# Two transformer layers: row maxima moved SBUF to SBUF, expert weights rounded by GpSimd, and an output projection moved into the tail of linear attention

## The reference

```python
# layer 0: softmax attention with alibi, 16 heads of 32
xn = layernorm(x)
q, k, v = split(xn @ Wqkv + bqkv, 3)
scores = q @ k.T / sqrt(32) - slope[h] * (i - j), causal
att = softmax(scores) @ v
x = x + att @ Wo + bo + moe(xn)            # two experts, W0a/W0b and W1a/W1b, top 1
# layer 1: linear attention with decay, gate and group norm
xn = layernorm(x)
q, k, v = silu(xn @ Wq), silu(xn @ Wk), silu(xn @ Wv)
S_t = exp(ld) * S_{t-1} + k_t v_t^T;  o_t = q_t S_t
o = o * sigmoid((xn @ Wg1) @ Wg2)
o = o * rsqrt(mean(o*o per head) + eps) * norm_w
x = x + o @ Wo + glu(xn)                   # glu with weights rounded to -1, 0, 1
```

## Time and profile before

| | us |
|---|---|
| median of 3 runs | 1733.5 (1728.63 to 1733.7) |
| the profiled execution | 1733.02, span 1731.2, mean granted clock 0.955 |
| TensorE busy in the span | 1556.5 (90%) |
| VectorE, ScalarE, GpSimd busy | 989.4, 603.2, 647.9 |
| attention | 167.4 to 805 |
| linear attention | to 1474.5, first matmul of `glu` at 1476.76 |

### The profile page before, as it was taken

One profiled execution on the slowest core, in us unless ns is written; L12 is line 12 of the kernel. 1 busy time (PEld: TensorE's weight loads), 2 busy tenths in 40 slices (PEclk: granted clock), 3 DMA queues, 4 the chain that ended last, 5 costly groups with the idle time before them and its releaser, 6 DMA issues. The chain is left out here.

```text
span 1731.2 us, 22070 instructions
## 1 busy us (share of the span) xinstructions
PE 1556.5 (90%) x7890; PEld 1080.1 (62%) x7890; DVE 989.4 (57%) x1698; ACT 603.2 (35%) x1137; POOL 647.9 (37%) x530
## 2 busy tenths in 40 slices
PE   5998769999999999996979999839999996999997
PEld 4886434444545555543757777737777774788886
DVE  7764857778877888762435555445654445222232
ACT  3221225555555555554212122144424222222221
POOL 4000033376788677784336666523120201000000
PEclk9998879999999999998989999959999997999999
DMA  6876503645545375224741211153030105320210
GB/s 229 264 232 205 118 4 86 128 104 103 129 119 113 78 180 116 57 87 132 242 140 55 67 56 58 52 186 128 1 122 1 50 31 152 116 98 1 98 49 25
DMA packets 103257, 182.28 MB, mean 105 GB/s; under 512 B 29018, under 2 KB 45290, under 8 KB 101274
## 3 DMA queue, kind: packets, MB, share of 16 engines
q1 hardware_dynamic: 85636, 121.39, 25.6%
q0 software_dynamic: 13648, 51.61, 10.0%
q10 hardware_dynamic: 3866, 7.87, 1.4%
HBM read 118.83 MB, written 62.02 MB: 104 GB/s over the span
## 5 line engine op out<-in xcount | busy, mean ns | idle before, releaser
L999 ACT ACTIVATE att_probs<-att_ring 128x512 f32<-128x512 f32 (+3 forms) x640 | 298.8, 537 | 295.5 <-DVE att_ring L1036 154.5
L1027 DVE TENSOR_REDUCE att_maxes<-att_ring 128x2 f32<-128x1024 f32 (+7 forms) x366 | 338.7, 946 | 68.2 <-PE att_ring L921 58.0
L956 PE MATMUL att_outp<-att_probs,att_vs 128*64 128x512 f32 (+3 forms) x1280 | 276.1, 553 | 0.3 <-ACT att_att L982 0.3
L956 PEld LDWEIGHTS att_outp<-att_probs,att_vs 128*64 128x64 f32 x1280 | 79.6, 139 | 122.0 <-issue 70.8
L942 PE MATMUL att_ring<-route_wah,route_wbh 102*128 102x512 f32 (+2 forms) x320 | 106.1, 408 | 13.4 <-ACT att_probs L999 7.3
L921 PE MATMUL att_ring<-route_wbh,route_wah 100*128 100x512 f32 (+2 forms) x320 | 103.8, 406 | 14.7 <-PEq L57 6.4
L921 PE MATMUL att_ring<-moew_wbl,moew_wal 100*128 100x512 f32 (+2 forms) x320 | 98.7, 384 | 17.2 <-ACT att_probs L999 9.0
L1685 DVE TENSOR_TENSOR glu_hid<-glu_sig,glu_u 128x512 f32<-128x512 f32 x44 | 30.2, 687 | 139.0 <-ACT glu_sig L1663 139.0
L1700 POOL DMA_DIRECT2D out<-glu_y x4 | 3.1, 787 | 278.2 <-DVE glu_y L1691 278.2
L942 PEld LDWEIGHTS att_ring<-route_wah,route_wbh 102*128 102x128 f32 x320 | 55.5, 194 | 76.1 <-issue 44.3
L942 PE MATMUL att_ring<-moew_wal,moew_wbl 102*128 102x512 f32 (+2 forms) x320 | 100.4, 399 | 2.4 <-DVE att_maxes L1027 2.3
(11 more groups left out here) (270 smaller groups left out, 3516.0 us busy)
## 6 DMA issues: line engine op xcount, KB each, us to landing
att_q_raw<-in_w POOLq DMA_DIRECT2D x48, 352.0 KB, 4.1
w_ternary<-att_q_out POOLq DMA_DIRECT2D x24, 352.0 KB, 2.7
tail_up<-w_ternary SPq DMA_DIRECT2D x22, 256.0 KB, 4.9
xn<-qkv_x SPq DMA_DIRECT2D x4, 1024.0 KB, 7.8
q_hi<-qkv_hi SPq DMA_DIRECT2D x16, 256.0 KB, 3.9
q_lo<-qkv_lo SPq DMA_DIRECT2D x16, 256.0 KB, 4.5
k_hi<-qkv_hi SPq DMA_DIRECT2D x16, 256.0 KB, 2.9
k_lo<-qkv_lo SPq DMA_DIRECT2D x16, 256.0 KB, 3.9
```

Of the source, the lines that this page charges most:

```text
L956: last = pe.matmul(outp[v_cols(h), off:CH], vs[p % 2][:, kt, v_cols(h)], probs[:, g % 4, h, off:CH], start=kt == 0, stop=kt == TT * (c + 1 ...
L999: act.activation(probs[:, g % 4, h, off:CH], ring[:, rg.banks["score", g][h], off:CH], ACT.Exp).then_inc(exped, 1)
L1027: last = dve.tensor_reduce(maxes[:, hs, t, g:g + 1], banks[:, :, 0:width], AX.X, ALU.max)
```

## The change

Three edits.

1. *Row maxima.* `store_rows` and `fetch_rows` become `move_rows`: for each head and each of 4 blocks one DMA straight from `rows` into `qs`, 8 per group, all on SyncE (of group 0 half on ScalarE), one step after the maxima are made. The DRAM tensor goes. VectorE's reuse of `rows` and TensorE's first score of a group wait for all 8 (`row_in`, `ROW_MOVES`). Pair 1's queries and keys are loaded by GpSimd, after group 1's moves have landed, with a semaphore of their own (`second_in`); its values by SyncE at step 16.
2. *Expert weights.* `hi_by`: GpSimd rounds each piece itself, right before it subtracts. ScalarE's roundings in this stage go.
3. *Linear attention.* The output projection of chunk 2 leaves chunk 3 and goes to the tail: two of its four tiles ahead of the mean squares, two between these and the spreading. The squares of chunk 3 are made per 128 tokens. Chunk 3's rows are loaded again into `x`, which takes the place of `y` in the buffer that the next stage reads, so that `y` keeps chunk 2's until it is stored at the end.

```diff
@@ WeightSplit
+    def hi_by(self, pool, j):
+        src, hi, lo = self.pieces[j]
+        pool.wait_ge(self.loaded[j % self.depth], 16 * (j // self.depth + 1))
+        pool.tensor_copy(hi, self.stage[j % self.depth][:, 0:src.shape[-1]]).then_inc(self.hi_done, 1)
@@ attention_stage
-        def store_rows(eng, n):
+        def move_rows(eng, n, heads=(0, 1)):
+
+            p, c = divmod(n, NCH)
             eng.wait_ge(rows_ready, n + 1)
-            for r in range(2 * 2):
-                eng.dma_start(rows_d[n, r, :].rearrange("(t b q) -> b t q", t=TT, q=HD), rows[n % 2][r:P:HD, :, :]
-                              ).then_inc(rows_stored[n % 2], 16)
-
-        def fetch_rows(eng, n):
-            p, c = divmod(n, NCH)
-            eng.wait_ge(rows_stored[n % 2], (n // 2 + 1) * 64)
-            eng.dma_start(qs[p % 2][SROWS:SROWS + 2, :, c * CH:(c + 1) * CH].bitcast(F32),
-                          rows_d[n].rearrange("(a h) q -> a h q", h=2)).then_inc(row_in[n % 2], 16)
+            for h in heads:
+                to = qs[p % 2][SROWS:SROWS + 2, h, c * CH:(c + 1) * CH].bitcast(F32).rearrange("a (t b q) -> a t b q", t=TT, q=HD)
+                for b in range(P // HD):
+                    eng.dma_start(to[:, :, b, :], rows[n % 2][b * HD + h:b * HD + h + 3:2, :, :]).then_inc(row_in[n % 2], 16)
@@ sync
-            store_rows(sp, 1)
-            fetch_rows(sp, 1)
-            sp.wait_ge(row_in[1], 16)
-            queries(1, first)
-            queries(1, late)
-            keys(1, whole)
-            load_values(sp, 1)
+            move_rows(sp, 0, (0,))
+            move_rows(sp, 1)
             for g in range(NG):
...
+                if g == SECOND_VALUES_AT:
+                    load_values(sp, 1, v_in[1])
@@ scalar
-            store_rows(act, 0)
-            fetch_rows(act, 0)
+            move_rows(act, 0, (1,))
...
-                for n in range(NN):
-                    if fetched_at(n) == g:
-                        fetch_rows(act, n)
-                piece, between = divmod(g - SPLIT_FROM, SPLIT_EVERY)
-                if g >= SPLIT_FROM and not between and piece < len(ahead):
-                    ws.hi(act, piece)
@@ gpsimd
-            pool.wait_ge(exped, 1)
+            pool.wait_ge(row_in[1], ROW_MOVES)
+            queries(pool, 1, first, second_in)
+            queries(pool, 1, late, second_in)
+            keys(pool, 1, whole, second_in)
             for j in range(ws.depth):
                 ws.load(pool, j)
             router.store(pool)
             for j in range(len(ahead)):
+                ws.hi_by(pool, j)
                 ws.lo(pool, j)
@@ lightning_stage, sync
+                if c == NCH - 1:
+                    sp.dma_start(x[:], rows_of(x_d, c)).then_inc(last_in, 16)
+                    continue
...
             sp.wait_ge(made, rg.made("gk", NCH - 1))
             for f in range(GT):
                 kept.load(sp, up_d, f)
+            wait_taken(sp, "out", NCH - 2, TT - 1)
+            sp.dma_start(rows_of(out_d, NCH - 2), y[:]).then_inc(stored, 16)
+            sp.wait_ge(stored, (NCH - 1) * 16)
@@ lightning_stage, tensor
-                if c:
+                if c and c + 1 < NCH:
                     output(c - 1)
...
+            output(NCH - 2, range(0, TT // 2))
             mean_squares(NCH - 1)
+            output(NCH - 2, range(TT // 2, TT))
             spread_inverses(NCH - 1)
             output(NCH - 1)
@@ lightning_stage, scalar
+                    if c + 1 == NCH and t:
+                        square_block(t - 1)
-            square(NCH - 1)
+            square_block(TT - 1)
@@ lightning_stage, vector
+            add_output(NCH - 2, range(0, TT // 2))
             invert(NCH - 1)
+            add_output(NCH - 2, range(TT // 2, TT))
             normalize(NCH - 1)
             add_output(NCH - 1)
```

More of the change, by code:

```diff
@@ L811, in attention_stage @@
         pair_in = [st.sem(f"pair_in{i}") for i in range(2)]
-        v_in, row_in, rows_stored = ([st.sem(f"{n}{i}") for i in range(2)] for n in ("v_in", "row_in", "rows_stored"))
+        v_in, row_in = ([st.sem(f"{n}{i}") for i in range(2)] for n in ("v_in", "row_in"))
+        second_in = st.sem("second_in")
         unit_made, unit_masked, unit_taken = st.sem("unit_made"), st.sem("unit_masked"), st.sem("unit_taken")
@@ L855, in _, with queries, keys @@
+        def queries(eng, p, t, arrived):
+            load_queries(eng, qs[p % 2], p, t, qh_d, ql_d, aq_d, arrived)
+        def keys(eng, p, t, arrived):
+            load_keys(eng, ks[p % 2], p, t, kh_d, kl_d, ak_d, arrived)
+        first, late, whole = slice(0, T - CH), slice(T - CH, T), slice(0, T)
         @block.sync
         def _(sp):
[L857 to L861, removed]
@@ L863, in _ @@
-            first, late, whole = slice(0, T - CH), slice(T - CH, T), slice(0, T)
             def store(p, c):
@@ L915, in unit_product @@
                 if p and v % NS == 0:
[L916 removed]
+                    if p == 1:
+                        pe.wait_ge(second_in, 3 * LOADS * 16)
+                    else:
+                        pe.wait_ge(pair_in[par], p // 2 * 3 * LOADS * 16)
                 out = [ring[:, b, :] for b in rg.banks["unit", v]]
@@ L1721, in __init__ @@
                                       ("norm", TT, -1), ("out", TT, 1), ("turn", KT, 0)):
+                if kind == "out" and c == NCH - 1:
+                    continue
+                if kind == "out" and c == NCH:
+                    order += [(kind, NCH - 2, n) for n in range(count)]
                 if 0 <= c - late < NCH:
@@ L1780, in lightning_stage @@
         root, inv, tmp = gk, st.sb("inv", [P, CH]), st.sb("tmp", [P, CH])
-        y, x = kept.y, st.sb("x", [P, TT, D])
+        y, x = st.sb("y", [P, TT, D]), kept.y
         def rows_in(n, k):
@@ L1885, in mean_squares @@
             def mean_squares(c):
-                pe.wait_ge(squared, c + 1)
+                pe.wait_ge(squared, c + 1 if c + 1 < NCH else c + TT)
                 pe.wait_ge(fresh_ready, (c + 1) * TT)
@@ L1899, in spread_inverses, with output @@
                 last.then_inc(spread_made, 1)
-            def output(c):
+            def output(c, ts=range(TT)):
                 if c == 0:
@@ L1904, in output @@
                 pe.wait_ge(lo_ready, (c + 1) * KT)
-                for t in range(TT):
+                for t in ts:
                     out, s = slot("out", c, t), slice(t * P, (t + 1) * P)
@@ L2140, in norm_low, with add_output @@
                                       xh[:, :, s].bitcast(F32), ALU.subtract).then_inc(taken["dve"], 1)
-            def add_output(c):
-                dve.wait_ge(r_in, c * 16 + 16)
-                for t in range(TT):
-                    dve.tensor_tensor(y[:, t, :], y[:, t, :], arrived(dve, "out", c, t), ALU.add
+            def add_output(c, ts=range(TT)):
+                if c == NCH - 1:
+                    dve.wait_ge(last_in, 16)
+                else:
+                    dve.wait_ge(r_in, c * 16 + 16)
+                to = x if c == NCH - 1 else y
+                for t in ts:
+                    dve.tensor_tensor(to[:, t, :], to[:, t, :], arrived(dve, "out", c, t), ALU.add
                                       ).then_inc(taken["dve"], 1)
@@ L2200, in _ @@
                     norm_low(c + 1)
-                if c:
+                if c and c + 1 < NCH:
                     add_output(c - 1)
-                else:
+                elif c == 0:
                     ws.wait(dve)
```

47 lines of the change are left out of this document (24 added, 23 removed).

## The result

| | us |
|---|---|
| before, median of 17 runs of that comparison | 1734.9 (1728.6 to 1742.2) |
| changed kernel, median of 17 runs | 1722.3 (1701.0 to 1729.3) |
| ratio to before | 0.9882, 95% interval 0.9855 to 0.9909 |
| profiled execution after | 1729.3, span 1727.5 |

The kernel is faster by 1.2%: 20.5 us by the ratio, where 23 had been predicted. The changed kernel's times lie 28 us apart, twice as far as those of before, and the profiled execution is the slowest of them. Its trace therefore shows what goes wrong in a bad run. What a part is worth is read from the ratios of the experiments, not from this one span.

A forecast was written before the change was run, and what follows sets the result against it. TensorE was taken to set mid-attention's pace, with DMA waits at its start and the output projection in linear attention's path. 8.9 + 2.6 + 1.0 + 10.1 + 0.3 = 22.9 us off 1733.0 gave 1710 us, range 1697 to 1721.

The forecast's parts named there:

- Linear attention, 10.1 + 0.3: Last chunk: moving chunk 2's output projection starts the recurrence 10.1 us earlier; filling the tail's gaps gains a net 0.3 us.
- The start, 8.9: Start of attention: the wait for group 2's row maxima goes, 7.3 us, plus 1.6 us of clock; bounds 0 and 8.9.
- Pair 1's twelve loads go to GpSimd's queue, so group 2's moves can be issued: Start of attention: freeing SyncE's queue lets group 2's moves be issued at 199.6 us, when its maxima are there.
- Rival C: The hole from 234 to 262 us goes too, through the maxima's traffic: 12 us more, 1698 us; chance 0.14.
- GpSimd's rounding, 2.6 + 1.0: Attention: ScalarE loses 16 roundings; 2.6 us at the stall near 317 us, 1 us from other fetches and roundings.
- GpSimd's own bill ... Cost nothing, hidden behind TensorE's products: Attention: 10 us more GpSimd work costs nothing; pieces end at 321, last quantization store issues near 762 us.
- B: Rival: attention's start doesn't pay, as pair 1 comes late or group 2's moves are stuck; 1721 us, chance 0.12.
- D: Rival: moves of later groups arrive after the score product needing them, 5 us a pair; slower, 1745 us, chance 0.03.
- E: Rival: GpSimd becomes the bound, pieces taking 98 us, so attention ends as today; 1722 us, chance 0.03.

The follow-up runs named there:

- act_rounds: Changed kernel, but ScalarE rounds the expert weights' upper halves at the steps of before; ratio to before 0.9874.
- lin_only: Kernel before with the linear attention part of the change alone; ratio 0.9938, median 1723.5 us.
- run 9: after_sync_pair: changed kernel, copy and subtraction kept, with pair 1's queries and keys issued by SyncE; ratio 0.9766, median 1697.6 us.
- run 8: links_sync_pair: changed kernel with four VectorE reductions replacing reduction, copy and subtraction, and pair 1's queries and keys on SyncE; ratio 0.9747, median 1688.8 us.
- run 11: values_late: the kernel of run 8, but every later pair's values load at step 16; ratio 0.9724, median 1689.4 us.
- att_only: Kernel before with all of the change except the linear attention part; ratio 0.9976, median 1735.7 us.
- reduce_links: Changed kernel with four VectorE reductions replacing the row maxima's reduction, copy and subtraction; ratio 0.9788, median 1698.3 us.
- links_act: Run 6: changed kernel with the four reductions and ScalarE rounding the expert weights as before; ratio 0.9854, median 1708.0 us.
- both: Changed kernel with the four reductions, the router's 16 indirect stores spread one ahead of each expert piece; ratio 0.9765, median 1693.5 us.
- moves_alone: Run 10: kernel before with only the row maxima's moves and pair 1's values at step 16; ScalarE rounds, SyncE loads pair 1; ratio 0.9924.
- run 4: reduce_links: changed kernel with four VectorE reductions replacing the row maxima's reduction, copy and subtraction; ratio 0.9788, median 1698.3 us.
- run 5: before_links: kernel before with the four reductions replacing reduction, copy and subtraction, nothing of the change; ratio 0.9983.
- spread_sync: The kernel of run 8 with the router's 16 indirect stores spread over the expert pieces; ratio 0.9762, median 1698.5 us.
- run 7: both: changed kernel with the four reductions, the router's 16 indirect stores spread one ahead of each expert piece; ratio 0.9765, median 1693.5 us.
- run 12: spread_sync: the kernel of run 8 with the router's 16 indirect stores spread over the expert pieces; ratio 0.9762, median 1698.5 us.

## Why: the steps of the prediction against the runs

**Linear attention, 10.1 + 0.3: right**, by the ratio (10.7) and step by step. From the start of the last matmul ahead of the output projection to the gate product it takes 1416.61 - 1415.48 = 1.1 us; before it was 0.2 more than the 1420.64 - 1409.62 = 11.0 of the earlier trace rows: 10.1 gained. In the tail the mean squares start 1443.38 - 1437.78 = 5.6 us after the recurrence's last product ends, 1.6 later than before (forecast 1.5). From that end to the last projection it is 19.9 us; before, 1461.98 - (1445.80 - 4.00) = 20.2: 0.3 gained.

**The start, 8.9: size about right, one edit in it wrong.** Moves and pair 1 on GpSimd together are act_rounds less lin_only: (0.9938 - 0.9874) x 1734 = 11.1 us; in the trace it is 8.3 us up to pair 1. An issue took 5.31 us for 8 moves, where 4.5 had been taken from the stores. But the step "Pair 1's twelve loads go to GpSimd's queue, so group 2's moves can be issued" named the wrong cause. With the same loads on SyncE (runs 8 to 10) nothing is held: the moves go out as early. And the same edit costs: put back on SyncE it gives 20 us in the changed kernel (run 9) and 9.5 us with the reductions (run 8). The hold of 15.03 us in the earlier trace rows stood behind the queries, the keys *and* the values. The change also moves the values to step 16, and run 11 shows that this ends the holds at the later pairs. I read a full queue rightly and charged the wrong part of what filled it.

What the GpSimd loads cost shows as the hole. In all five kernels with the moves and pair 1 on SyncE, TensorE is busy from 234 to 262 us; of the six with pair 1 on GpSimd it has the hole in four (after, att_only, act_rounds, reduce_links), and not in links_act and both (one trace each). The kernel before has the hole too, with pair 1 on SyncE and the maxima through DRAM. The router's indirect stores run at the same beat of 1.27 us in all but the spread ones, so they alone are not the cause, and neither are the copy and subtraction, since reduce_links has the hole. Rival C, which let the hole go through the maxima's traffic, is thus true of moves_alone but not of the changed kernel. In the hole VectorE starts long after the product that it waits for is listed as ended:

```profile
239.02 0.63 PE L920 MATMUL att_ring<-moew_wbl,moew_wal 100*128 100x512 f32 x2
...
241.36 0.43 DVE L1015 TENSOR_TENSOR att_ring<-att_ring,route_cst 128x256 f32<-128x256 f32 x1 [3.08 <-DMA qkv_wstage<-in_Wqkv]
...
242.57 0.44 PE L941 MATMUL att_ring<-route_wah,route_wbh 102*128 102x384 f32 x1 [2.27 <-issue]
...
249.85 0.50 DVE L1028 TENSOR_TENSOR att_ring<-att_ring,route_cst 128x128 f32<-128x128 f32 x2 [7.33 <-DMA qkv_wg<-in_Wg]
```

The addition at 241.36 is 1.7 us behind the product that ends at 239.65, the one at 249.85 is 6.8 us behind that of 243.01; the releasers that the profile names are loads of a stage long past. Why GpSimd's loads bring this about stays open. The Trainium skill's advice weighed in the prediction ("SBUF — State Buffer", section "SBUF: two separate sides") is to issue from ScalarE or SyncE instead. It points the right way, but what it warns of, a late load, is not what the trace shows: pair 1 was there at 221.53.

**GpSimd's rounding, 2.6 + 1.0: the failed step.** In the changed kernel it gave nothing: 0.9882 with it, 0.9874 without. "GpSimd's own bill ... Cost nothing, hidden behind TensorE's products" counted GpSimd's line alone. It left out what GpSimd does to VectorE. Run 4 shows a price: 16 us come back once VectorE's copy and subtraction are reductions. That GpSimd's instruction holds VectorE's copy back is shown by removal (in all seven kernels with reductions none of the 64 lasts over 0.3 us), and by the rows above in time. The Trainium skill states it, in "SBUF — State Buffer", section "Who interferes with whom": a copy or cast in a two-port mode, and a two-input operation with both inputs in SBUF against GpSimd's reads, wait for GpSimd's whole instruction, while a reduction never does. Trace and runs agree: 2371, 1658 and 172 ns at most. I used that page of the Trainium skill for GpSimd's descriptors and not for VectorE's own 64 short operations, whose stretched rows stood in the trace of before already.

How much of the 16 us is the waits and how much the clock and the keys that follow from them was not measured apart. In the profiled run the waits on maxima and exponentials from 262 us on are 15.3 us, against 10.3 in the kernel before and 1.9 in reduce_links.

But the 16 us are not the price of the stretched copies wherever they stand. With pair 1 on SyncE the same reductions take the ratio from 0.9766 (run 9) to 0.9747 (run 8), 3 us with overlapping intervals, although in run 9 GpSimd rounds and 9 of the 64 still last over 1 us; its waits on `att_maxes` are 3.0 us. In the kernel before they gave nothing that can be told (run 5). Reductions alone give 16 us, pair 1 on SyncE alone 20, both 23: what the stretch costs depends on when GpSimd's work meets VectorE's, and why pair 1's place changes that was not found.

Once either is mended, the rounding is worth far more than 3.6: 9.7 us between the medians of runs 6 and 4, and about 17 between moves_alone with lin_only (0.9924 x 0.9938 = 0.9863) and after_sync_pair (0.9766), which differ in it alone and where copy and subtraction stand as they were. The term was sized by the stall of 3.39 us at 317.87. But the hole ahead of it had covered ScalarE's earlier roundings; where the hole goes, they cost 10.7 and 13.8 us. Two terms that I added were not independent.

**Balance.** By ratios: linear attention 10.7, moves with the later values 13.2, rounding 17, less 20 for pair 1 on GpSimd, is 20.9; measured 20.5. (The last two entries share run 9, so this closes by the way it is set up and proves nothing.) The forecast of 1710 (0.987 of before) met the ratio of 0.988 with a sum in which an overlooked loss and a gain booked too small cancelled. Linear attention's term held and so, in size, did the start's; that the rest cancelled was luck.

**The rivals.** B (pair 1 late, 1721): its place was wrong, for nothing there was late, though ten of the 17 runs gave its time or more. D (late moves): no score product of the changed kernel waits for a move. E (GpSimd the bound): refuted by 766.08.

**Better than both kernels** is links_sync_pair: the change, four reductions in place of the three links, pair 1 on SyncE: 1684.2 to 1691.2 us, 2.5% under before, with values_late its equal. Nearly all of its gain over the changed kernel comes with pair 1 alone (run 9).

## What to carry to other kernels

Before work is moved to GpSimd, list VectorE's copies and two-input operations in SBUF and look at their maximum beside their median: where a few stretch to the length of a GpSimd instruction, more GpSimd work can make more of them do so (8 of 64 here before, 14 after; 9 with pair 1 on SyncE). Turned into reductions they stopped; whether that brings time depends on the rest of the kernel, so measure it both ways.

A hold in a DMA queue names the DMA that is stuck, not the one to be moved; try first to postpone the one that is needed last. And when a stall is sized from the trace of before, ask what the idle time ahead of it hides: if another term removes that, the stall grows.

## What the runs showed that I had not expected

A VectorE copy of 8 columns took up to 2371 ns beside GpSimd work and 174 at least. The kernel with 14 such events in its trace scatters over 28 us and reduce_links over 6, but that these events make the scatter is not shown: spread_sync, with reductions, scatters over 14 us in 6 runs, and act_rounds, with the copies, over 6 in 4. TensorE fell to 1.2 GHz for a while behind waits of only 1.28 to 2.19 us (five times in the profiled run between 421 and 705 us, at a mean grant of 0.91 in those stretches of 20 us), so that a short wait costs more than itself, though not each time (a wait of 1.28 us at 577.6 had no fall behind it): the sums of 8 matmuls that follow the wait at 421.48 took 3.24 us, the next 1.94.

```profile
422.68 3.24 PE L955 MATMUL att_outp<-att_probs,att_vs 128*64 128x512 f32 x8
...
427.69 1.94 PE L955 MATMUL att_outp<-att_probs,att_vs 128*64 128x512 f32 x8
```

And 12 loads moved from GpSimd's queue to SyncE's took away a stretch of late starts on VectorE, ScalarE and TensorE, 30 us after the loads' traffic had ended.
